# VectorE adds all four quarters of a batch's exponentials, in place of two additions on GpSimd and one on VectorE

## The reference

```
logits = (einsum('tzd,ed->tze', x, phi_w) + phi_b).reshape(t, z, n=64, p=32)
D = softmax(logits, axis=3)          # over the slots of an expert
C = softmax(logits, axis=2)          # over the experts, for each slot
X_tilde = einsum('tznp,tzd->npd', D, x)      # summed over all batches
X_tilde = tanh(layernorm(clip(X_tilde)))
Y_tilde = einsum('npd,ndH->npH', X_tilde, expert_w) + expert_b
Y = einsum('tznp,npH->tzH', C, Y_tilde)      # then x = x + Y
# fourth layer, per batch: W from cond; q, k, v; rope; softmax attention; Wo;
# rmsnorm; swiglu; router over 8 experts; rmsnorm
```

## Time and profile before

| | us |
|---|---|
| median of three runs | 1158.93 (1158.67 to 1160.22) |
| profiled execution | 1161.0 |
| its span | 1159.1 |
| TensorE busy | 1024.4 (88%) |
| VectorE busy | 757.3 (65%) |
| ScalarE busy | 517.2 (45%) |
| GpSimd busy | 158.1 (14%) |

### The profile page before, as it was taken

How to read it: one execution, slowest core, us unless ns; L and a number is a source line. 1 busy time by engine, 2 the same in 40 slices (tenths; PEclk the granted TensorE clock), 3 DMA queues, 4 the chain that set the end, 5 groups by cost and what they waited for, 6 DMA issues and landing times.

```text
span 1159.1 us, 18222 instructions
## 1 busy us (share of the span) xinstructions
PE 1024.4 (88%) x6734; PEld 766.1 (66%) x6760; DVE 757.3 (65%) x1831; ACT 517.2 (45%) x835; POOL 158.1 (14%) x166
## 2 busy tenths in 40 slices
PE   4989999998758899999999973879999999999876
PEld 3878888887546667776767643656657666666543
DVE  4475555554474778888888885464576756768646
ACT  2255444435332554474467422114736464554251
POOL 1120110100038200000000004012021220202000
PEclk9999999999688999999999985889999999999998
DMA  8000000000110221011300003000000000000000
GB/s 328 2 28 15 15 15 15 14 15 1 49 79 1 103 80 55 4 53 55 128 1 1 1 1 110 1 1 1 1 1 6 1 6 6 1 5 1 6 5 10
DMA packets 11800, 35.39 MB, mean 31 GB/s; under 512 B 2570, under 2 KB 5818, under 8 KB 10944
## 3 DMA queue, kind: packets, MB, share of 16 engines
q1 hardware_dynamic: 10464, 33.14, 8.1%
q10 hardware_dynamic: 1152, 1.05, 0.3%
q0 software_dynamic: 96, 0.04, 0.0%
HBM read 33.16 MB, written 1.06 MB: 30 GB/s over the span
## 4 chain that ended last, share of the span: by engine, by line
PE 60%; DVE 15%; issue 15%; DVEq 4%; ACT 3%; POOL 1%; POOLq 1%; another core or an unknown queue 0%; ACTq 0%
PE ps L1134 5%; PE ps L850 5%; PE ps L1120 5%; PE ps L1061 3%; PE ps L1016 3%; PE ps L1280 3%; PE ps L1195 3%; PE ps L1175 3%; PE ps L1213 2%; PE ps L884 2%; DVE arena L1855 2%; PE ps L1036 2%; PE ps L860 2%; PE ps L896 2%; PE ps L1009 2%
## 5 line engine op out<-in xcount | busy, mean ns | idle before, releaser
L1960 DVE TENSOR_REDUCE arena<-ps 128x8 f32<-128x2048 f32 x32 | 73.3, 2292 | 37.3 <-PE ps L1175 37.3
L1488 ACT ACTIVATE arena<-ps 128x2048 f32<-128x2048 f32 x32 | 60.1, 1879 | 57.5 <-PE ps L1199 57.5
L1120 PE MATMUL ps<-uR,arena 128*128 128x256 f32 x256 | 74.5, 386 | 0.1
L1061 PE MATMUL ps<-arena 128*128 128x128 f32 x512 | 67.8, 288 | 5.6 <-DVE arena L1871 4.8
L1061 PEld LDWEIGHTS ps<-arena 128*128 128x128 f32 x512 | 65.4, 203 | 10.9 <-issue 7.7
L1036 PE MATMUL ps<-arena,uR 128*128 128x512 f32 x128 | 68.7, 618 | 3.5 <-ACT arena L1433 3.0
L1134 PE MATMUL ps<-arena 128*128 128x256 f32 x256 | 65.6, 403 | 6.6 <-DVE arena L1941 3.7
L1461 ACT ACTIVATE arena<-ps 128x512 f32<-128x512 f32 x64 | 38.0, 599 | 61.3 <-PE ps L1121 54.9
L1280 PE MATMUL ps<-arena 128*128 128x512 f32 x128 | 62.1, 608 | 2.3 <-DVE arena L2026 0.9
L1134 PEld LDWEIGHTS ps<-arena 128*128 128x128 f32 x256 | 49.1, 199 | 20.5 <-issue 9.6
L850 PE MATMUL ps<-arena 128*128 128x256 f32 x256 | 58.5, 386 | 0.0
(11 more groups left out here) (388 smaller groups left out, 2324.6 us busy)
## 6 DMA issues: line engine op xcount, KB each, us to landing
arena<-in_skills SPq DMA_DIRECT2D x16, 768.0 KB, 5.6
arena<-in_expert_w SPq DMA_DIRECT2D x2, 2048.0 KB, 8.1
arena<-in_l_experts SPq DMA_DIRECT2D x8, 386.5 KB, 3.1
arena<-in_consts_b SPq DMA_DIRECT2D x1, 1152.0 KB, 9.4
x2R<-in_x ACTq DMA_DIRECT2D x8, 128.0 KB, 6.4
arena<-in_L_w SPq DMA_DIRECT2D x2, 512.0 KB, 11.8
arena<-in_phiC SPq DMA_DIRECT2D x1, 1024.0 KB, 12.7
arena<-in_expert_b SPq DMA_DIRECT2D x1, 1024.0 KB, 4.7
```

The costliest lines, as they stand in the source:

```text
L1061: last = mm(high[:, 2, t * P:(t + 1) * P], eD[h][:, k, col:col + P], uT[u][:, k, :], start=k == 0, stop=k == 1)
L1120: mm(o, phiC[:, st_ * P:(st_ + 1) * P], uR[:, b, :], start=True, stop=False)
L1488: av(pexp[:, t, gp].rearrange("p c h t -> p (c h t)"), scores[:, :, :].rearrange("p c t -> p (c t)"), ACT.Exp, scale=SCALE3).then_inc(s.sc ...
L1960: V.tensor_reduce(nm[:, k, :, 2 * gp:2 * gp + 2], scores[:, :, :].rearrange("p c (h t) -> p c h t", h=2), X, ALU.max, negate=True).then_in ...
```

## The change

GpSimd's steps CSA and CSB are taken out of its list, and the semaphore `cs_pool` and the tile `csA` go. VectorE's step CSUM adds the four quarters itself, in three additions of 128 x 1024 values with a drain (`dr()`) between them, and then folds as before. It still begins with the wait for the eighth exponential.

```
-                    dve.wait_ge(s.cs_pool, at(b, 2, 1))
                     dve.wait_ge(s.eC_ready, at(b, 8, 7))
-                    V.tensor_tensor(csF, csA, eC[u][:, 12:16, :].rearrange("p a t -> p (a t)"), ALU.add)
+                    quarter = [eC[u][:, 4 * j:4 * j + 4, :].rearrange("p a t -> p (a t)") for j in range(4)]
+                    V.tensor_tensor(csF, quarter[0], quarter[1], ALU.add)
+                    dr()
+                    V.tensor_tensor(csF, csF, quarter[2], ALU.add)
+                    dr()
+                    V.tensor_tensor(csF, csF, quarter[3], ALU.add)
                     dr()
...
-                if n == "CSA":
-                    pool.wait_ge(s.eC_ready, at(b, 8, 3))
-                    if b > 0:
-                        pool.wait_ge(s.csum_ready, at(b - 1))
-                    G.tensor_tensor(csA, eC[u][:, 0:4, :].rearrange("p a t -> p (a t)"),
-                                    eC[u][:, 4:8, :].rearrange("p a t -> p (a t)"), ALU.add).then_inc(s.cs_pool, 1)
-                if n == "CSB":
-                    pool.wait_ge(s.eC_ready, at(b, 8, 5))
-                    pool.drain()
-                    G.tensor_tensor(csA, csA, eC[u][:, 8:12, :].rearrange("p a t -> p (a t)"), ALU.add).then_inc(s.cs_pool, 1)
```

More of the change, by code:

```diff
@@ L251 @@
     W.0 WA.0 W.1 RSZ.0 WA.1 W.2 WA.2 W.3 RSZ.1 WA.3 W.4 WA.4 W.5 WA.5 RSZ.2 W.6 WA.6 W.7 WA.7 RSZ.3 RSZ.4 RSZ.5
-    RSZ.6 RSZ.7 VZ.0 CSA.0 JR0.0 CSB.0 JR1.0 QM.0 CSA.1 CSB.1 QM.1 CSA.2 CSB.2 RS1.0 QM.2 CSA.3 CSB.3 RS1.1
-    RS2.0 QM.3 CSA.4 RS1.2 CSB.4 RS2.1 QM.4 CSA.5 RS1.3 CSB.5 RS2.2 QM.5 CSA.6 RS1.4 CSB.6 RS2.3 QM.6 CSA.7
-    CSB.7 RS1.5 RS2.4 QM.7 RS1.6 RS2.5 RS1.7 RS2.6 RS2.7""",
+    RSZ.6 RSZ.7 VZ.0 JR0.0 JR1.0 QM.0 QM.1 RS1.0 QM.2 RS1.1
+    RS2.0 QM.3 RS1.2 RS2.1 QM.4 RS1.3 RS2.2 QM.5 RS1.4 RS2.3 QM.6 RS1.5 RS2.4 QM.7 RS1.6 RS2.5 RS1.7 RS2.6 RS2.7""",
 }
@@ L381, in __init__ @@
         self.eC_ready = sem("eC_ready")
-        self.cs_pool = sem("cs_pool")
         self.csum_ready = sem("csum_ready")
@@ L650, in build @@
         w3raw = sb("w3raw", [P, E, P])
-        csA = w3raw[:, :, :].rearrange("p a d -> p (a d)")
         wave = cst[:, CONSTS["cos"][0]:CONSTS["sin"][1]]
```

## The result

| | before | changed |
|---|---|---|
| median of the runs, same chip | 1159.28 us (1158.67 to 1160.22, 4 runs) | 1179.87 us (1179.32 to 1181.84, 4 runs) |
| ratio, 95% interval | 1 | 1.018 (1.0162 to 1.0198) |
| profiled execution, span | 1161.0, 1159.1 us | 1179.3, 1177.5 us |
| VectorE busy, GpSimd busy | 757.3, 158.1 us | 773.2, 125.2 us |

The change makes the kernel 20.6 us slower. The forecast was 1178 with 1171 to 1185. A second set of runs, beside other runs of the kernel before, gave 1.0186 (1.0161 to 1.0211). All 72 runs of the kernel before in this document lie between 1154.4 and 1162.6 us, 17 of them up to 1156.7 and the others from 1158.0 on; each kernel but the changed one has one profile, so places read from a profile are those of one execution.

The account below looks back on a forecast made before the run. TensorE bounds the second pass, with CSUM's folds on its path. Stalls 17.2 - junction 2.4 + clock 4 = 18.8 us on the profiled 1161.0 gives 1179.8; with the median 2.1 lower, 1178, range 1171 to 1185.

Parts of the forecast that it names:

- The bound and the path: Second pass: TensorE is the bound, and VectorE's CSUM folds lie on its path with at most 0.1 us slack.
- The stalls: Batches 1 to 7: two added VectorE additions, 2.60 us a batch, delay TensorE's CSUM matmul; 17.2 us in all.
- rival C: Batches 3 to 7: half the delay absorbed by hidden TensorE slack, no loss of clock; 1168 us, chance 0.05.
- The junction's gain: Batch 0: without GpSimd's additions VectorE's clip and JB are no longer held up, so Y starts 2.4 us earlier.
- The bounds, 0.9 to 3.4: Batch 0's gain in us: from JM's gain alone, 0.9, to the whole shift of ScalarE's tanh, 3.4.
- The clock: Half clock behind about two stalls of batches 3 to 6, 3.4 us, plus 0.6 in batches 1 and 2; together 4.
- The term that was most under-sized: Batch 2's clock loss: already at half behind its waits; 0.6 us together with batch 1, at most 1.5 each.
- Rival B: Every stall drops TensorE's clock, costing 10 us; 1183.7 us, chance 0.19.
- rival A: The stalls are there but TensorE's clock stays up; 1173.7 us, chance 0.22.
- Rival E: The two new VectorE additions are slower than 1.23 us, their output being an input too; 1185 or more, chance 0.01.
- Rival D: GpSimd's additions hold VectorE up in every batch, 3.4 us each, so removing them gives 1149 us; chance 0.03.
- The signs: Changed profile: VectorE busy about 16 us more, GpSimd 35 less, TensorE's fold waits 21 in total, CSUM spacing 51.2 or 53.

Follow-up runs that it names:

- experiment 4: Against the kernel before: all additions on VectorE, in batches 1 to 7 one behind the fourth exponential, one right ahead of CSUM, one in CSUM; 1166.36 us, ratio 1.0058.
- experiment 8: The changed kernel with two additions in CSUM, the third quarter left out of the sum; 1166.41 us, ratio 1.0071 to the kernel before.
- experiment 9: The kernel before without GpSimd's additions; VectorE adds only first and fourth quarter, the others left out of the sum; 1157.72 us, ratio 0.998.
- experiment 1: Against the kernel before: VectorE adds all four quarters in batch 0 only, GpSimd adds as before in batches 1 to 7; 1155.71 us, ratio 0.9977.
- experiment 5: All additions on VectorE, two of three placed early in batches 1 and 4 to 7, but batches 2 and 3 as in the kernel before; 1159.94 us, ratio 1.0007.
- experiment 2: Against the kernel before: the change in batches 1 to 7 only, batch 0 keeping GpSimd's additions; 1181.90 us, ratio 1.0208.
- experiment 6: Against the kernel before: VectorE adds all four quarters in batch 2 only; 1165.24 us, ratio 1.0041.
- experiment 7: Against the kernel before: VectorE adds all four quarters in batches 4, 5 and 6 only; 1169.69 us, ratio 1.0081.
- its repeat: The changed kernel run and profiled once more, unaltered, beside the same runs of the kernel before; 1180.81 us, ratio 1.0186.
- experiment 3: Against the kernel before: batch 0's three additions on VectorE ahead of the junction, batches 1 to 7 as before; 1154.43 us, ratio 0.9966.

## Why the prediction was right, and where it was not

**The bound and the path: right.** CSUM's folds are on TensorE's path in every batch from 1 on. That was read from a slack of 0.1 us in the earlier trace rows, and the changed kernel's waits and experiments 4, 8 and 9 agree: one addition, one step of spacing.

**The stalls: right.** Forecast 17.2, measured 16.8. Batches 1 to 3 grew by 2.53 each (4.63, 3.65 and 3.09 for 2.10, 1.12 and 0.56), 4 to 6 by 2.5, batch 7 by 1.7 to the wait of 1.74. Nothing else took it back, so rival C is out.

**The junction's gain: the step of it that failed is the second half.** Forecast 2.4 us earlier for Y, measured 1.1. The first steps came: clip 0.69, L1904 0.13 and 0.16, the tanh 3.6 earlier (forecast 3.4), the second tanh 1.4 earlier (forecast 0.9). Then JM was to end 0.9 earlier, and it ended 0.3 later (22.5 us behind the clip for 22.2). The working had taken TensorE's durations from the kernel before. But ahead of the second JX TensorE now waits for the copy for 3.07 us (1.31 before), and the second JX and the start of JM run at half clock: 1.94 and 4.48 us for 1.07 and 3.70, which is 1.7 us. The experiments bear it out: in the four kernels with three additions between the two JB (the changed one, experiments 1, 4 and 5) TensorE waits 3.07 there and the two take 6.4 us together, in the seven others it waits 1.25 to 2.21 and they take 4.8. The bounds, 0.9 to 3.4, held it.

**The clock: about the right size, in other places.** Forecast 4, from half clock behind about two of the stalls of batches 3 to 6 and 0.6 in batches 1 and 2. Measured in batches 1 to 6: 5.7, of which 0.9 + 3.2 in batches 1 and 2 and 1.6 behind batch 3, and nothing in batches 4 to 6. Another 1.7 lies in the tail. On the other side stand 3.0 us given back in batch 0, which the forecast didn't have: Y and the start of batch 1 ran at full clock where they hadn't. Experiment 2 shows that the 1.7 in Y can come without any edit to the junction; that it never failed to come in the seven kernels with the edit speaks for a part of the change in it, but doesn't settle it. With all of them the clock's net is 4.4 where 4 was forecast, out of terms that mostly weren't the forecast's: that is partly luck.

The term that was most under-sized is batch 2. It was put at 1.5 at the most, on the ground that it was at half clock already. In the kernel before that was 3 us; now the clock is at half for 13 us. TensorE waits 3.65 us and, one matmul later, 2.04 for X5; but a wait for X5 stood there before too, of 2.22, and the length at half doesn't follow from the waits alone: some 14 us with a fold's wait of 1.65 (experiment 4), some 10 with 3.65 (experiment 6), some 7 with 1.12 (experiment 1). Experiments 4 and 5 show that later folds in batches 2 and 3 cost more than their length there; why the clock stays down for so long is not shown. The Trainium skill, "TensorE: Matmul & The Clock Gate", section "HAM oscillation — how this bites in real kernels", says of waits between bursts that each burst then starts cold. The waits that it describes are longer than the stalls of 2.26 us, so it doesn't decide about them. For the longer ones it holds: the ten waits for a fold of 3.09 to 4.63 us (the changed kernel, its repeat, experiments 2 and 6) had the clock at 1.00 in the 2 us before them and at 0.50 or 0.51 in the 2 us behind them. Of the twelve of 2.26 us (the first three and experiment 7) one was followed by half clock. Nine of the ten and nine of the twelve come from kernels that are the same from batch 1 on. Rival B is out by the changed kernel's batches 4 to 6, rival A by its batches 2 and 3. Rival E is out too: each of the additions takes 1.23.

**Rival D: refuted by its own measure.** GpSimd's additions hold VectorE up in the junction, where they meet a clip or a small operation with all operands in SBUF. In the other batches they cost 0.1 us at most (experiment 9). What VectorE ran beside them there had an operand in PSUM; the 15 of the 32 reductions (L1960) among it took as long as the other 17.

**The signs.** VectorE busy +15.9 (forecast +16). GpSimd -32.9 (forecast -35): the eight pairs were 34.8, and the powers of RS1 took 1.9 longer, eight of 1.06 us on average for 0.81, now that VectorE adds beside them. In the kernel before and the changed one:

```profile
L2179 POOL TENSOR_TENSOR arena<-arena,half_neg 128x2 f32<-128x2 f32 x8 | 6.5, 812 | 1.2
```

```profile
L2170 POOL TENSOR_TENSOR arena<-arena,half_neg 128x2 f32<-128x2 f32 x8 | 8.4, 1056 | 1.2 <-issue 0.2
```

TensorE's waits for the fold: 19.9 (forecast 21; batch 0 has none, and the slack in batches 4 to 6 came off). Spacing of batches 4 to 7: 51.2, as forecast for those without loss of clock.

**What stays open.** Why one stall of 2.26 us in twelve was followed by half clock, and whether Y's full clock belongs to the change. And why the wait of 1.97 us in the tail is followed by half clock in one execution and not in another. It was in seven of the twelve profiles (the changed kernel and its repeat, experiments 2, 3, 4, 6 and 9), whose tails took 103.5 to 104.2 us, and not in the other five, with 101.6 to 102.5; no relation to the edits shows.

## What to carry to other kernels

Time on an engine with room to spare costs nothing only where nobody waits for it: three additions of 1.30 us in a row behind the last producer moved the end by their whole length in each batch, though GpSimd's two were slower and the sum of engine time fell. Put partial sums where their inputs are ready and the engine idles; with the same additions on the same engine, placed early, the steady cost fell from 2.5 to 0.75 us a batch, and in batch 0 three early additions gave the lowest median, though its interval overlaps that of experiment 1. When a stall is walked through a timeline, the durations behind it must be asked about too: those of TensorE were for the other level of its clock.

## What the runs showed of the hardware

- A GpSimd addition of 128 x 1024 beside VectorE stretched the second clip of 128 x 1024 in SBUF from 0.69 to 2.65 us, and an operation on 8 values a partition from 0.13 to 1.75; the second ended as GpSimd's addition did, the clip 0.5 us behind it. It was so in all four kernels with these additions in batch 0, and in none of the seven without. Reductions of 128 x 2048 from PSUM took 2.28 to 2.29 us either way: in the kernel before 15 of the 32 overlap an addition.
- It works in the other direction: GpSimd's power of 8 values took 1.66 us beside VectorE's statistics (L1897) and 2.48 beside its additions, in the changed kernel's junction:

```profile
709.27 1.66 POOL L2133 TENSOR_TENSOR arena<-arena,half_neg 128x8 f32<-128x8 f32 x1
711.93 2.48 POOL L2133 TENSOR_TENSOR arena<-arena,half_neg 128x8 f32<-128x8 f32 x1
```

- The same stall of 2.26 us kept the clock at 2.4 GHz in eleven cases and lost it in one; those of 3.09, 3.65 and 4.63 lost it in all ten, with the clock at 1.00 in the 2 us before; the tail's wait of 1.97 was followed by half clock in seven profiles of twelve. So the length of a wait alone doesn't tell whether the clock falls. In the two profiles of the changed kernel the places were the same; between the profiles of different kernels they moved, into stretches that no edit touched, and the 72 runs of the kernel before differ by up to 8 us.
